# Attention of one graph with the other layers of its neighbours spread into its slots

## The chip, the cores and the metric

One Trainium2 chip; the program uses one of its cores. The metric is the device time of one execution in microseconds. Engines are named as in the profile: PE (TensorE; PEld its weight loads), DVE (VectorE), ACT (ScalarE), POOL (GpSimd), SP (SyncE, which here issues every DMA).

## What is computed

Sixteen graphs of N = 1024 nodes with D = 256 features go through two layers, each with a residual. `adj` holds 0 or 1 here (about 3% ones, and the diagonal), though the kernel also serves values up to 4.

```python
# layer 0: 8 heads of 32
h = maximum(layernorm(x), 0)
Q, K, V = h @ Wq.T + bq, h @ Wk.T + bk, h @ Wv.T + bv        # split into heads
A = softmax(where(adj == 0, -inf, Q @ K.T * HD**-0.5))       # per head, 1024 x 1024
x = x + concat(A @ V) @ Wo.T + bo
# layer 1: one "head", the score depends on the edge's kind
h = maximum(layernorm(x), 0)
e_k = leaky_relu((h * a_k) @ h.T, 0.2)                       # k = 0..3
s = where(adj == k + 1, e_k, ...), else -9e15
x = x + softmax(s) @ h
```

With ones only, `e_0` alone is needed. A flag per graph (is any entry above 1?) chooses at run time between that and a general path; on these inputs the general path is never taken.

## The kernel before

**Tiles.** A graph's attention is 64 tiles of 128 rows of scores by 1024 columns (8 heads x 8 row blocks; the order is four heads of a block, then the next block, and after 32 tiles the other four heads). Each tile is one *slot* of the loop in `layer0`: PE writes the scores into one of two PSUM tiles `ps` (`scores`, L837, two products over 96 rows: high and low parts of Q and K are stacked so that one product gives the split-precision sum); DVE adds the mask `bias` and takes the row minimum (`mask`, L510) into `sm`; ACT takes the exponential (L349); PE transposes the tile in eight pieces into `pT[0]` and `pT[1]` (L856); ACT copies the first half to `pt` (L359) and DVE the second (L525). `pt` has eight tiles (`SLOTS`). The attention values of a group of four tiles (64 weight loads and products, L873) are spread over four slots, a quarter behind the transposes of each (`values(t // HG - 1, t % HG)`). Scores run two slots ahead. Every 16 tiles (a quad) DVE forms row factors (L532, L535), PE transposes them (L884), ACT copies them (L365) and DVE scales the values into `ot` (L546).

**Order of a graph** (`graph`, L992 on PE, and the same on each engine, written out by hand): attention (`layer0`); transposes of the next graph's normalized `xf` (L778); `output` (L908, 32 products); the next graph's `front`: four products qk of twelve instructions (K and Q for heads 0 to 3, then for 4 to 7; L773), whose high parts ACT and low parts DVE write to a staging area in `pt` (L341, L469), and the value products; then `layer1`: h1 transposed (L778, L379, L592), and for each of eight tiles `edges` (12 products L773 of the row block scaled by a_0, whose parts L602, L387 and L611 make), DVE mask (L667) and leaky ReLU (L674), ACT exponential (L397), transposes (L963), copies (L403, L685), values with h1 (L975) and the result (L690, L693). `layer1` ends with the first two scores of the next graph.

**SP** issues in one queue: x1 and xf loads, the stacks (`stacks`, L220: 48 copies of staged parts into `ks` and `qs`), then adjacency halves (L208, 256 KB each, two buffers) for the next graph's masks beside layer 1, and the stores of the result.

**POOL** turns each adjacency half into `bias` with one pass (L290), adds the output bias to x1 (L308), and normalizes xf (`front_norm`, L297, L298, L302). **DVE** takes the maximum of every adjacency half (L483) for the flag. The next graph's statistics (L448) are taken on DVE in slots 22 to 30 of the attention.

## Time and profile before

| | |
|---|---|
| three runs, median (lowest to highest) | 3982.55 us (3978.19 to 3991.47) |
| profiled execution, span from first to last instruction (the page gives no other time of it) | 3976.3 us |
| mean granted TensorE clock | 0.967 |
| busy PE, DVE, ACT, POOL | 3669.7, 3128.6, 2267.1, 674.9 us |
| chain that ended last, by engine | PE 68%, SP queue 11%, issue 9%, DVE 7%, DMA 2%, ACT 1% |
| instructions | 94630 |

Busy time is the union of an engine's instructions. PE's is modelled at its ends, so a high share does not mean that PE works at its peak. "Issue" is time in which an engine waited for nothing that the profile shows. Of two consecutive instructions of one engine the second can start a little ahead of the end of the first, so what an instruction costs in a full queue is the distance of the two starts.

### The profile page before, as it was taken

The page shows a single profiled execution, that of the slowest core. Times are in us where ns is not written, and L with a number is a line of the kernel's source. Part 1 is how long each engine was busy: PE and PEld are TensorE (multiplying, and loading weights), DVE is VectorE, ACT ScalarE, POOL GpSimd, SP SyncE. Part 2 cuts the span into 40 slices and gives each one's busy share as a digit, 9 for nine tenths or more (in the row PEclk, how much of TensorE's full clock was granted, in tenths as well). Part 3 has the DMA queues.
Part 4 walks back from the last instruction along what each step waited for, and adds up shares of the span by engine and source line. Part 5 has one row for each costly group of instructions (what it writes and reads, how often), then busy time and mean ns, then how long its engine had stood idle before and what let it go on. Part 6 is the DMA issues. An engine that isn't in the chain of part 4 may idle for free.

```text
span 3976.3 us, 94630 instructions
## 1 busy us (share of the span) xinstructions
PE 3669.7 (92%) x34096; PEld 2908.9 (73%) x34096; DVE 3128.6 (79%) x5926; ACT 2267.1 (57%) x3940; POOL 674.9 (17%) x440
## 2 busy tenths in 40 slices
PE   6989989899998989989899898998989989899998
PEld 5777777777777767777777777776777767777776
DVE  6968778687886978869788696886968869688785
ACT  3837547275573845738456384663836638366482
POOL 1021030310303103031020301203012030120300
PEclk8999999999999999999999999999999999999999
DMA  5041220403204032040310503104031040311300
GB/s 151 2 105 36 60 82 2 117 25 70 71 2 118 23 76 66 2 131 10 81 61 4 137 2 83 59 15 126 2 89 53 21 121 2 95 47 31 99 2 12
DMA packets 129070, 227.67 MB, mean 57 GB/s; under 512 B 20672, under 2 KB 71104, under 8 KB 128448
## 3 DMA queue, kind: packets, MB, share of 16 engines
q1 hardware_dynamic: 128448, 219.50, 20.3%
q8 instruction: 376, 6.16, 0.7%
q14 instruction: 246, 2.02, 0.2%
HBM read 101.98 MB, written 16.78 MB: 30 GB/s over the span
## 4 chain that ended last, share of the span: by engine, by line
PE 68%; SPq 11%; issue 9%; DVE 7%; DMA 2%; ACT 1%; DVEq 0%; POOL 0%; POOLq 0%; ACTq 0%
PE pT L856 21%; PE ps L837 15%; PE pO L873 13%; SPq L220 11%; PE ps L773 8%; PE pO L975 7%; PE pT L908 2%; DMA adj_half<-in_adj_dram 2%; PE pT L963 2%; DVE pt L525 1%; DVE most L483 1%; DVE sm L667 1%; PE pO L884 1%; DVE sm L510 1%; DVE sm L674 1%
## 5 line engine op out<-in xcount | busy, mean ns | idle before, releaser
L349 ACT ACTIVATE sm<-sm,mn 128x1024 f32<-128x1024 f32 x1024 | 1179.5, 1152 | 454.8 <-DVE mn L510 452.5
L510 DVE CUSTOM_DVE_ANT_0 sm<-ps,bias 128x1024 f32<-128x1024 f32 x1024 | 1250.9, 1223 | 197.5 <-PE ps L837 178.0
L856 PE MATMUL pT<-ident,sm 128*128 128x128 f32 x8192 | 1098.6, 276 | 40.3 <-DVE pt L525 37.1
L856 PEld LDWEIGHTS pT<-ident,sm 128*128 128x128 f32 x8192 | 961.3, 142 | 218.5 <-DVE pt L525 52.8
L837 PE MATMUL ps<-ks,qs 96*128 96x512 f32 x2048 | 754.4, 451 | 4.6 <-issue 3.7
L525 DVE COPY pt<-pT 128x512 f32<-128x512 f32 x1024 | 702.4, 686 | 31.5 <-PE pT L856 30.8
L873 PE MATMUL pO<-pt,v 128*32 128x128 f32 x16384 | 649.7, 278 | 4.8 <-DVE pt L525 4.8
L359 ACT COPY pt<-pT 128x512 f32<-128x512 f32 x1024 | 583.2, 570 | 56.7 <-PE pT L856 56.4
L290 POOL TENSOR_SCALAR bias<-adj_half 128x512 bf16<-128x512 int32 x240 | 468.0, 1950 | 864.3 <-DMA adj_half<-in_adj_dram 855.7
L873 PEld LDWEIGHTS pO<-pt,v 128*32 128x32 f32 x16384 | 388.2, 109 | 170.1 <-issue 170.1
L975 PE MATMUL pO<-h,pt 128*128 128x256 f32 x2048 | 463.0, 379 | 0.0
L837 PEld LDWEIGHTS ps<-ks,qs 96*128 96x128 f32 x2048 | 312.6, 191 | 179.0 <-issue 168.9
L975 PEld LDWEIGHTS pO<-h,pt 128*128 128x128 f32 x2048 | 380.5, 190 | 47.5
L387 ACT ACTIVATE ah<-hs,nacol 128x128 fp32r<-128x128 f32 x256 | 87.0, 393 | 545.8 <-DVE hs L602 458.9
L773 PE MATMUL ps<-hh,ah 128*128 128x512 f32 x512 | 243.8, 476 | 161.1 <-DVE al L611 161.1
L773 PEld LDWEIGHTS ps<-hh,ah 128*128 128x128 f32 x512 | 111.7, 218 | 204.7 <-DVE al L611 181.6
L313 POOL TENSOR_TENSOR rstd<-vpe,mhalf 128x8 f32<-128x8 f32 x16 | 26.2, 1638 | 1294.3 <-DVE vpe L579 1294.3
L483 DVE TENSOR_REDUCE most<-adj_half 128x1 f32<-128x512 int32 x256 | 164.6, 678 | 95.0 <-DMA adj_half<-in_adj_dram 94.9
L773 PE MATMUL ps<-hl,ah 128*128 128x512 f32 x512 | 223.9, 437 | 0.0
L773 PE MATMUL ps<-hh,al 128*128 128x512 f32 x512 | 222.5, 435 | 0.0
L667 DVE CUSTOM_DVE_ANT_0 sm<-ps,bias 128x1024 f32<-128x1024 f32 x128 | 155.7, 1217 | 66.4 <-PE ps L773 66.4
L397 ACT ACTIVATE sm<-sm,mnl 128x1024 f32<-128x1024 f32 x128 | 147.1, 1149 | 91.3 <-DVE sm L674 91.3
(104 smaller groups left out, 3526.5 us busy)
## 6 DMA issues: line engine op xcount, KB each, us to landing
adj_half<-in_adj_dram SPq DMA_DIRECT2D x256, 256.0 KB, 2.8
ks<-pt SPq DMA_DIRECT2D x384, 128.0 KB, 2.4
qs<-pt SPq DMA_DIRECT2D x384, 128.0 KB, 2.4
xf<-in_x_dram SPq DMA_DIRECT2D x16, 1024.0 KB, 8.0
x<-in_x_dram SPq DMA_DIRECT2D x16, 1024.0 KB, 5.7
out_dram<-x SPq DMA_DIRECT2D x128, 128.0 KB, 2.9
x<-in_L_gnn_Wq_dram SPq DMA_DIRECT2D x1, 256.0 KB, 2.8
x<-in_L_gnn_Wk_dram SPq DMA_DIRECT2D x1, 256.0 KB, 3.1
```

The source lines that it names most:

```text
L220: sp.dma_start(dst[HD * row:HD * (row + 1), HG * (q // 2) + h, :].bitcast(F), stage[HD * h:HD * (h + 1), q, part, :].bitcast(F)).then_inc( ...
L290: nc.gpsimd.tensor_scalar(bias[:, t, c * HALF:(c + 1) * HALF], adj_half[:, c, :], 0.0, BIG, ALU.is_equal, ALU.mult).then_inc(mask_made, 1)
L349: nc.scalar.activation(sm[:, t % RING, :], sm[:, t % RING, :], ACT.Exp, scale=-1.0, bias=mn[:, t:t + 1], accum_out=den[:, t:t + 1]).then_i ...
L359: nc.scalar.copy(pt[:, t % SLOTS, 0:NT // 2, :], pT[0][:, :].rearrange("p (m n) -> p m n", n=P)).then_inc(pt_made[0], 1)
L483: nc.vector.tensor_reduce(most[:, i:i + 1], adj_half[:, i % 2, :], AX, ALU.max, apply_absolute_value=True).then_inc(adj_most, 1)
L510: nc.vector.tensor_tensor_reduce(out=sm[:, t % RING, :], in0=ps[t % 2][:, :], in1=bias[:, node, :], scale=1.0, scalar=3e38, op0=ALU.add, o ...
L525: nc.vector.tensor_copy(pt[:, t % SLOTS, NT // 2:, :], pT[1][:, :].rearrange("p (m n) -> p m n", n=P)).then_inc(pt_made[1], 1)
L773: last = nc.tensor.matmul(out, a, c, start=start and i == 0, stop=stop and i == len(terms) - 1)
L837: last = nc.tensor.matmul(ps[t % 2][:, c * HALF:(c + 1) * HALF], qs[:, head, node * P:(node + 1) * P], ks[:, head, c * HALF:(c + 1) * HALF ...
L856: last = nc.tensor.transpose(pT[c][:, j * P:(j + 1) * P], sm[:, t % RING, m * P:(m + 1) * P], ident[:, :])
L873: last = nc.tensor.matmul(pO[quad % 2][HD * h:HD * (h + 1), n], v[:, m, o:o + HD], pt[:, (HG * g + h) % SLOTS, m, :], start=(m == 0), stop ...
L975: last = nc.tensor.matmul(pO[t % 2][:, 0:D], pt[:, t, m, :], h1[:, m, :], start=(m == 0), stop=(m == NT - 1))
```

## The change

The kernel is reorganized so that a *stage* b is the attention of graph b, and all other work is cut into units that stand in its slots. On PE a slot is now: scores of tile s + 2; where it is due, a group's values (all 64 at once) and row transposes; the transposes of tile s; then the slot's unit, if it has one. Units share the two PSUM tiles `ps` with the scores in turn. For graph b itself: value products (slots 1, 2) and qk for heads 4 to 7 (4, 6). For the graph before, o = b - 1: output (3, 5), transposes of h1 (10, 11), and eight edge tiles (13, 17, ... 41), whose transposes follow three slots later ahead of the values of the group, and whose values stand in two halves ahead of the transposes of the two slots behind these. For the graph after: front transposes (53, 55) and qk for heads 0 to 3 (57, 58). DVE and ACT have the same slots; each engine's work on a unit stands behind its copy of the slot.

Buffers: `pt` has four tiles and one for layer 1 (before eight); h1 is `xf`; one PSUM tile `pA` holds the attention values, one, `pB`, row factors, layer 1 values and the flag; layer 1 has one `sm` slot and its own bias `gbias`. Adjacency is loaded twice per graph, for the masks and again for layer 1. The maximum on DVE is gone; POOL sums the excess over 1 instead. The sums L602 and the scalings L387, L611 per tile are replaced by one scaling of all of h per k. The relu of h1 is one ACT pass per block with the norm in it. Stacks are issued per head, for heads 4 to 7 of graph b behind slots 4 and 6, for heads 0 to 3 of the next behind slot 58.

```diff
-SLOTS = 8
+def background(earlier, later):
+    units = {1: ("value", 0), 2: ("value", 1), 4: ("qk", 2), 6: ("qk", 3)}
+    if earlier:
+        units.update({3: ("out", 0), 5: ("out", 1), 10: ("h", 0), 11: ("h", 1)})
+        units.update({13 + 4 * t: ("edge", t) for t in range(NT)})
+    if later:
+        units.update({53: ("front", 0), 55: ("front", 1), 57: ("qk", 0), 58: ("qk", 1)})
+    return units
...
-        pt = sb("pt", [P, SLOTS, NT, P], F)
+        pt = sb("pt", [P, HG + 1, NT, P], F)
...
# SP
+            def stack_heads(f, heads):
+                for h in heads:
+                    for q in range(2):
+                        dst = (ks, qs)[q]
+                        for row, part in enumerate(((0, 1, 0), (0, 0, 1))[q]):
+                            sp.dma_start(dst[HD * row:HD * (row + 1), h, :].bitcast(F),
+                                         parts[HD * h:HD * (h + 1), 2 * q + part, :].bitcast(F)
+                                         ).then_inc(stacked[h], 16)
+            def stage(b, later):
+                o, base = b - 1, 2 * NT * b
+                edge_adj(o, 0, base)
+                second_stack(b)
+                edge_adj(o, 1, base)
+                for t in range(NT - 3):
+                    edge_adj(o, t + 2, base)
+                    if t < NT - 4:
+                        store(o, t)
...
+                if later:
+                    mask_adj(b + 1, 3, base)
+                    sp.wait_ge(pv, NT * (o + 1))
+                    settle(sp)
+                    load_xf(b + 1, 0)
+                    load_xf(b + 1, 1)
+                store(o, 7)
...
+                load_x1(b)
+                if later:
+                    mask_adj(b + 1, 5, base)
+                    mask_adj(b + 1, 6, base)
+                    sp.wait_ge(s_mm, TILES * b + TILES // 2)
+                    settle(sp)
+                    first_stack(b + 1, (0, 1))
+                    mask_adj(b + 1, 7, base)
+                    stack_heads(b + 1, (2, 3))
# POOL
+            def masks(f, node, loaded):
+                for c in range(2):
+                    half = bias[:, node, c * HALF:(c + 1) * HALF]
...
+                        nc.gpsimd.tensor_scalar(half, adj_half[:, c, :], 1.0, 0.0, ALU.subtract,
+                                                ALU.max).then_inc(over_half, 1)
...
+                        nc.gpsimd.tensor_tensor(over[:, :], over[:, :], half, ALU.add).then_inc(over_sum, 1)
...
+                    nc.gpsimd.tensor_scalar(half, adj_half[:, c, :],
                                             0.0, BIG, ALU.is_equal, ALU.mult).then_inc(mask_made, 1)
+            def next_masks(f, node):
+                pool.wait_ge(masked, TILES * (f - 1) + TILES // 2 + HG * (node + 1))
...
+                masks(f, node, 2 * NT * (f - 1) + mask_load(node))
...
+                if later:
+                    next_masks(b + 1, 0)
+                    edge_bias(o, NT - 1, base + edge_load(NT - 1))
+                    for node in range(1, 5):
+                        next_masks(b + 1, node)
                     front_norm(b + 1)
+                    next_masks(b + 1, 5)
+                    residual(b)
+                    next_masks(b + 1, 6)
+                    next_masks(b + 1, 7)
# DVE, one slot
+                for s in range(TILES):
+                    if s + 2 < TILES:
+                        mask(b, s + 2, banks["score", s + 2], not earlier)
...
+                    if earlier and 16 <= s < 16 + 4 * NT and s % 4 == 0:
+                        edge_copy(o, (s - 16) // 4)
+                    if earlier and 19 <= s < 19 + 4 * (NT - 1) and s % 4 == 3:
+                        result(o, (s - 19) // 4)
...
+                    copy(b, s, not earlier)
+                    kind, n = units.get(s, ("", 0))
...
+                    if kind == "edge":
+                        edge_leaky(o, n)
+                    if s % 16 == 15:
+                        row_factors(b, s // 16, not earlier)
...
+                    if s and s % 16 == 0:
+                        norm(b, s // 16 - 1)
...
+                    if later and s in (48, 49):
+                        front_stats(b + 1, s - 48)
+                    if later and s == 49:
+                        front_aggregate(b + 1)
# PE, one slot
+                    if s + 2 < TILES or later:
+                        if s - 1 in units:
+                            pe.wait_ge(masked, TILES * b + s + 2)
+                        elif s - 2 in units:
+                            released(b, units[s - 2])
+                        else:
+                            pe.wait_ge(masked, TILES * b + s + 1)
...
+                    if earlier and 16 <= s < 16 + 4 * NT and s % 4 == 0:
+                        pe.wait_ge(pt_made[0], TILES * b + s)
+                        pe.wait_ge(pt_made[1], TILES * b + s)
+                        edge_transposes(o, (s - 16) // 4)
+                    if earlier and 18 <= s < 18 + 4 * (NT - 1) and s % 4 >= 2:
...
+                        edge_values(o, (s - 18) // 4, (s % 4 - 2,))
...
+                    if s and s % HG == 0:
+                        values(b, s // HG - 1, not earlier)
...
+                    transposes(b, s, not earlier)
+                    kind, n = units.get(s, ("", 0))
+                    if kind and s - 1 in units:
+                        released(b, units[s - 1])
+                    elif kind:
+                        pe.wait_ge(masked, TILES * b + s + 2)
+                    if kind == "value":
+                        value(b, n, banks["value", n])
...
# PE, the whole
+            stage(0, False, True)
             with pe.Fori(1, B - 1) as b:
-                graph(b, True)
+                stage(b, True, True)
+            stage(B - 1, True, False)
+            o = B - 1
...
+            edges(o, 0, 0, general)
+            for t in range(NT):
+                if t + 1 < NT:
...
+                    edges(o, t + 1, (t + 1) % 2, general)
...
+                edge_transposes(o, t)
+                edge_values(o, t, (0, 1))
```

`released` waits for the last reader of the unit's PSUM tile: for qk its low part on DVE, for h the low scaled part, for an edge tile its mask. `select`, the general path, is skipped by one branch per tile.

## Rows read from the trace of the kernel before

**Rows 1.** The page, part 1: busy time of each engine.

```profile
PE 3669.7 (92%) x34096; PEld 2908.9 (73%) x34096; DVE 3128.6 (79%) x5926; ACT 2267.1 (57%) x3940; POOL 674.9 (17%) x440
```

**Rows 2.** Windows: length, busy us of PE, PEld, DVE, ACT, POOL, clock, DMA share, GB/s.

```profile
0.00:62.00 62.00, 28.59 (x128) 24.28 (x128) 32.68 (x71) 9.58 (x10) 7.39 (x18) 0.81 0.55 157
1182.40:1428.10 245.70, 229.45 (x2130) 181.89 (x2130) 194.90 (x370) 141.54 (x246) 44.21 (x28) 0.97 0.21 58
1487.00:1494.00 7.00, 3.44 (x9) 2.73 (x10) 6.08 (x13) 2.30 (x5) 5.36 (x3) 0.52 0.27 83
3886.00:3976.30 90.30, 72.40 (x395) 60.92 (x384) 50.05 (x117) 23.60 (x45) 1.67 (x1) 0.91 0.04 14
```

**Rows 3.** Timeline of one attention slot and its neighbour. Columns: start us, us, engine.

```profile
1342.56 0.30 PEld L837 LDWEIGHTS ps<-ks,qs 96*128 96x128 f32 x2 [0.20 <-issue]
...
1342.91 1.02 PEld L856 LDWEIGHTS pT<-ident,sm 128*128 128x128 f32 x8
...
1343.52 1.23 DVE L510 CUSTOM_DVE_ANT_0 sm<-ps,bias 128x1024 f32<-128x1024 f32 x1
...
1344.10 0.38 PEld L873 LDWEIGHTS pO<-pt,v 128*32 128x32 f32 x16 [0.17 <-issue]
...
1344.67 0.69 DVE L525 COPY pt<-pT 128x512 f32<-128x512 f32 x1
1344.67 0.30 PEld L837 LDWEIGHTS ps<-ks,qs 96*128 96x128 f32 x2 [0.20 <-issue]
...
1344.79 1.15 ACT L349 ACTIVATE sm<-sm,mn 128x1024 f32<-128x1024 f32 x1 [0.36 <-DVE mn L510]
```

**Rows 4.** Timeline at the end of the same attention: last copy and value block.

```profile
1426.19 0.85 PEld L856 LDWEIGHTS pT<-ident,sm 128*128 128x128 f32 x8 [0.24 <-issue]
...
1427.32 0.69 DVE L525 COPY pt<-pT 128x512 f32<-128x512 f32 x1 [0.95 <-PE pT L856]
1427.93 0.24 DVE L532 RECIPROCAL rden<-den 128x16 f32<-128x16 f32 x1
1428.13 1.72 PEld L873 LDWEIGHTS pO<-pt,v 128*32 128x32 f32 x64 [0.54 <-issue]
...
1430.04 0.42 PEld L884 LDWEIGHTS pO<-ident,scratch 128*128 128x128 f32 x4 [0.20 <-issue]
```

**Rows 5.** Chain that ended last, one layer 1 step. Columns: start us, us.

```profile
1252.90 2.77 PE ps L773 x12
1255.68 0.87 PE pT L963 x8
1256.55 3.46 PE pO L975 x16
```

**Rows 6.** Groups of instructions by line, DVE and ACT, whole run.

```profile
L674 DVE SCALAR_TENSOR_TENSOR sm<-sm 128x1024 f32<-128x1024 f32 x128 | 156.0, 1219 | 0.0
...
L448 DVE BATCH_NORM_STATS2 st<-xf 128x6 f32<-128x256 f32 x128 | 52.9, 418 | 0.0
...
L379 ACT CAST hh<-ps 128x1024 fp32r<-128x1024 f32 x32 | 30.9, 1017 | 70.1 <-PE ps L778 70.1
```

**Rows 7.** Groups of instructions by line, POOL, whole run.

```profile
L290 POOL TENSOR_SCALAR bias<-adj_half 128x512 bf16<-128x512 int32 x240 | 468.0, 1950 | 864.3 <-DMA adj_half<-in_adj_dram 855.7
...
L302 POOL TENSOR_SCALAR xf<-xf,nmean,rstd 128x256 f32<-128x256 f32 x128 | 76.6, 611 | 3.5 <-POOL rstd L298 3.5
...
L308 POOL TENSOR_TENSOR x<-x,bob 128x2048 f32<-128x2048 f32 x16 | 73.2, 4574 | 209.6 <-DMA x<-in_x_dram 209.6
...
L298 POOL TENSOR_TENSOR rstd<-vpe,mhalf 128x8 f32<-128x8 f32 x16 | 26.7, 1666 | 0.0
```

**Rows 8.** Timeline of SP's queue: twelve stack copies, first to last issue.

```profile
1446.24 9.16 SPq L220 DMA_DIRECT2D ks<-pt  x12
```

**Rows 9.** The page, part 6: DMA issues, KB each, us to landing.

```profile
ks<-pt SPq DMA_DIRECT2D x384, 128.0 KB, 2.4
```

**Rows 10.** One line of the kernel: duration ns min/median/max.

```profile
L602 DVE TENSOR_TENSOR hs<-hh,hl x128: 410/419/832, 236.6 to 3950.1; 128x256 f32<-128x256 f32 x128
```

1451 lines of the change are left out of this document (771 added, 680 removed).

## The prediction

> **What bounds the kernel now.** The page's busy shares come first: PE is busy 92% of the span, DVE 79%, ACT 57%, POOL 17% [rows 1]. A busy share says little of where the time is lost, so I cut the run in windows. One graph takes 245.7 us; before the first graph's attention lie 62 us, after the last one's 90.3 us [rows 2]. The timeline of the attention shows a slot every 2.11 us, back to back on PE: scores .35, transposes 1.0 with a .17 gap behind them, a quarter of the values .38 and a .20 gap [rows 3]. So 64 slots are 135 us, bound by PE; DVE needs 1.75 of each slot (mask 1.15 from start to start, copy .60) [rows 3, 4], ACT about as much. The other 110 us of a graph are layer 1, whose steady step is 2.77 + .87 + 3.46 = 7.1 us on PE [rows 5], eight times 57 us, and output and front, 53 us in which PE has only some 31 us of work: four products of 2.77 (12 instructions of 512 columns, as the edges), 48 value instructions of half the width 5.7, 32 output instructions of .216 6.9 (3.46 for 16 of the same form), 32 transposes of .11 3.5, the row transposes 1.8, all from [rows 5] and the block in [rows 4]. The fourth window of [rows 2] shows what the waits there cost beside themselves: PE is busy 3.4 of 7 us and the granted clock is .52, the lower of the two levels (1.2 GHz). What the change can win is therefore at most the idle part of those 53 us.
>
> **The change, part by part.** The unit of account is one stage: 64 slots of attention with all units between. Constants, from start to start: S (scores) .35, T (transposes) 1.0, M (mask) 1.15, C (copy) .60; M can start .96 behind its S, the exponential 1.27 behind its M, C 1.13 behind its T [rows 3, 4].
>
> *Values in one lump.* pt shrinks from eight tiles to four and one for layer 1, and a group's 64 value instructions, before spread over four slots behind the transposes, now stand as one block ahead of the transposes of every fourth slot. On PE this is cheaper: 1.91 us as a block [rows 4] against four times .75. But the block needs all four copies, and the next copy needs the block. Four slots without a unit then are a ring: T to C 1.13, C .60, three times (M + C) 5.25, a hop of .2 (the block starts .81 behind the last copy's start), block 1.91, and .1 of waits: 9.2 us, where PE alone would need 4 x 1.35 + 1.91 = 7.3 and the kernel before takes 8.46. Cover is gone here: DVE has only one mask to do during the block.
>
> *Layer 1 in the slots.* A tile's step adds to four slots 2.77 of edges, 1.0 of transposes and 3.4 of values. PE sum: 4 x 1.35 + 1.91 + .17 + 2.77 + 1.0 + 3.4 = 14.6. Walking through the four slots, DVE (4 x 1.75, mask and leaky 2.4, copy and result 1.2 [rows 6]) is ready in time except for the last copy, on which the edge transposes wait .4. So 15.0 us, against 8.46 + 7.1 = 15.6 before. Eight times 15.0, two row transposes with their gaps 1.3, less .5 for the first tile: slots 13 to 44 take 121 us.
>
> *The other 32 slots.* I walked them in five stretches; each is the base of 9.2 per four slots or the PE sum, whichever is later, plus what is exposed.
> - Slots 45 to 52: base 18.4; the last tile's values 3.4; on DVE, which is the bound here, row factors .8, norm .6 (passes of the copy's size), eight statistics of .33 (.42 by their row [rows 6], overlapping by .09) 2.6, aggregates 1.0; the statistics stood at slots 22 to 30 before, in DVE's free .36 per slot. Sum 26.8.
> - Slots 53 to 58: base 13.8; two front transposes 2.0; two products qk 5.5; and a wait for POOL. POOL makes the next graph's masks with three passes per half where one was: two of 1.92 to 1.96 and a bf16 add of 512 columns that no row shows. The nearest rows bound it: 1.1 (a quarter of the 4.57 for 2048 columns) and 1.95 (the pass of the same size) [rows 7]; I take 1.2, as it is the same operation, and 5.2 per half with hops, 10.5 per node. Node 4 may start when slot 49's mask is done, 16.8 us into slot 45, ends at 27.4, and only then does front_norm follow (power 1.67 and small parts, 2.0, and four tiles of .61 [rows 7]): the front transposes of slot 53 can start at 31.9, PE is there at 27.9. Wait 4. Sum 25.3.
> - Slots 59 to 63 and slot 0: here SP is the bound. The stacks of the next heads are issued one after the other at .76 us (12 in 9.16 [rows 8]), 24 of them and two adjacency loads (1.2) behind the low parts of qk(1), the last lands 2.4 us later [rows 9]; the first needs 2.7 for the ACT and DVE passes on qk(1). 2.7 + 18.2 + 1.2 + 2.4 = 24.5. The jump back of the loop lies beside it.
> - Slots 1 to 6: PE sum 6 x 1.35 + 1.91 + values 5.7 + output 6.9 + qk 5.5 = 28.1, plus 2 of waits for the low parts (1.2, a pass of leaky's size [rows 6], behind ACT's 1.1) = 30.1.
> - Slots 7 to 12: base 13.8; both h units, each .9 on PE, two ACT passes of 1.02 [rows 6] and two DVE passes of 1.2, and each waited for before the next step: 11.2; the rest of qk(3) 1.2. Sum 26.2.
> Together 132.9. Walked slot by slot, some releases overlap with the base, 2.9 in all: 130.
>
> *What costs nothing.* Doubled adjacency loads (32 of 256 KB per stage): the DMA share is .21 [rows 2], and they go out between edges, 15 us apart. The vanished maxima, sums and scalings on DVE bring nothing either: DVE did them beside layer 1, where PE set the pace. Edge bias on POOL, 2 x 1.95, lies inside 15 us; if that cover went, the edge mask would be late. SP's second stack (24 issues, 18 us) ends just ahead of the scaled product in slot 10 that reuses its buffer.
>
> *Clock.* Waits of 4 us such as that of slot 53 stand in the trace ahead of stretches at 1.2 GHz; I add 1.7 for one such stretch. Nothing, and 5, are the ends.
>
> A stage: 121 + 130 + 1.7 = 252.7 us, where a graph takes 245.7. PE's own work falls to some 206 us (16 x 7.3, 57, 31), and it stands still for the other 47.
>
> *Ends.* Stage 0 has no layer 1; its masks are now POOL's alone, 10.5 us per node behind a slow SP queue, and it ends at 254 us (57 to the first slots instead of 62, masks of node 7 at 140, then 38 slots with the waits above). The last stage has no front: 22 less. The tail has one buffer for scores, values and copies in layer 1, so its step is T 1.0, copy .73, values 3.4, edges 2.77 = 7.9 for 7.1: 101 us instead of 90. Sum: 254 + 14 T + (T - 22) + 101 = 333 + 15 T = 4123 us with T = 252.7. The profiled execution has a span of 3976.3, the page gives no time around it, and the median of the runs is 6.3 us above it: **4130 us**, 3.7% slower.
>
> **Rivals.**
> 1. *PE stays the bound behind the block* (faster). If masks and copies keep up, for instance because PE's queue lets scores and transposes slip further ahead of DVE than I allow, four unit-free slots take 7.3 and not 9.2. Eight such groups: T = 252.7 - 15 = 237.5, total 3895 + 6 = 3900. It decides from T = 242.5 down, that is from 8.0 us per four slots. For it: the start-to-start times of M and C (1.75) fit into 2.11 with room; against it: DVE's ring is closed by the shrunken pt in the program itself, and at the end of each attention phase now, the block waits for the copy [rows 4]. Chance .20.
> 2. *The waits halve*: the transitions overlap better (units' low parts, POOL done earlier as its add is nearly free, stack DMAs earlier) and T lands at 242 to 243.5: no change, 3976 to 3988. Chance .05.
> 3. *POOL becomes the bound* (slower still). It works 44 us per graph now [rows 2] and would work some 135. TENSOR_TENSOR on DVE with both inputs in SBUF has a median of .419 but a longest of .832, [rows 10]: the two disturb each other already, rarely. If a half costs 7 in place of 5.2, the wait of slot 53 grows by 3.5, and the load ahead of the last stacks comes 6 later: T = 262, total 4270. Chance .13.
> The Trainium skill (SBUF, "Who interferes with whom") says that a DVE instruction with two SBUF inputs and a GpSimd instruction that reads SBUF exclude each other, the loser waiting for the whole instruction. By that rule each of the eight leaky passes could stand for a whole POOL pass and this rival would be the forecast. The trace bears it out only in part: the leaky pass of 1024 columns, two inputs in SBUF too, has a mean of 1219 ns over 128 [rows 6], beside POOL's mask passes of the same time.
> The forecast itself (ring of 9.2, T between 247 and 258, so 4045 to 4210) has .62.
> A further case, that the units do not run where the text puts them, I see no ground for: each engine's order is written out.
>
> **Numbers.** About .3%, 12 us, is what a measurement of this kernel can tell from no change. Faster .20, same .05, slower .75. The range takes the forecast's bounds, reaches down over half of rival 1 and rival 2, and up over most of rival 3: 3935 to 4240.
>
> **What would show it.** Right: in the new trace four unit-free slots (say 48 to 52 or 60 to 63) take over 9 us with V waiting on DVE's copy; four slots with an edge tile take near 15; PE waits for POOL's norm ahead of slot 53 and for stack DMAs at slots 63 and 0; value instructions stand in blocks of 64 in 1.9 us; PE's share falls under 88% in a longer span. Wrong: unit-free groups under 8 us; edge groups over 16 (then the layer 1 chain, not the transitions, is mis-sized); no wait at 53; a POOL busy share over 65%.

## The result and the profile after

The changed kernel takes 4325.2 us (median of 4 runs, 4319.3 to 4333.9) against 3987.0 for the kernel before on the same chip: 1.085 times as long, 95% interval 1.082 to 1.089. The forecast was 4130 us, range 3935 to 4240: the direction was right, the size 195 us short, and the result lies outside the range.

The page, part 1, of the changed kernel, to be held against [rows 1]:

```profile
span 4321.5 us, 94909 instructions
PE 3672.0 (85%) x34096; PEld 3013.0 (70%) x34096; DVE 2817.8 (65%) x4998; ACT 2245.5 (52%) x3812; POOL 2064.1 (48%) x1208
```

PE is busy for as long as before (3669.7), with the same number of instructions; DVE has 311 us less to do, POOL 1389 more. So PE stands for 343 of the 345 us more. The equal busy time hides two opposite things. By the trace's clock records PE was busy at 1.2 GHz, the lower of its two levels, for 28.6 us of a looped stage, and for 11.8 us of a graph before. An estimate from that, with matmuls that take twice as long at the lower level: at full clock PE would be busy for 213.5 us a stage where a graph took 222.9. The change did remove 9 us of work from the engine that bounds the kernel; the lower clock took 8 of them back (14.3 us for 5.9), and idle time grew by 18 (35.2 for 16.9).

I cut the run where DVE copies slot 0 of each stage (line L686). Stage 0 runs to 284.3, fourteen looped stages follow to 3967.2, 263.1 us each (of the kernel before, graph to graph: 245.7), and the last stage and the tail take 354.3. The windows of one looped stage, cut at the copies of slots 0, 6, 12, 16, 44, 48, 52, 58 and the next 0; the columns are those of [rows 2]:

```profile
1335.80:1367.00 31.20, 29.37 (x228) 24.83 (x226) 20.91 (x40) 12.41 (x21) 4.80 (x3) 1.00 0.25 59
1367.00:1391.20 24.20, 16.82 (x206) 13.69 (x206) 16.97 (x27) 18.36 (x31) 0.54 (x1) 0.93 0.36 89
1391.20:1409.10 17.90, 15.17 (x129) 12.21 (x128) 11.22 (x20) 9.03 (x17) 4.84 (x2) 0.81 0.10 32
1409.10:1517.70 108.60, 104.80 (x986) 87.89 (x985) 79.01 (x139) 60.84 (x107) 51.86 (x26) 1.00 0.15 49
1517.70:1530.30 12.60, 11.84 (x125) 9.71 (x124) 9.14 (x17) 7.35 (x14) 11.04 (x8) 1.00 0.44 132
1530.30:1545.00 14.70, 10.44 (x108) 7.92 (x106) 11.34 (x30) 6.90 (x13) 13.14 (x9) 0.77 0.42 131
1545.00:1570.10 25.10, 18.84 (x156) 15.29 (x155) 14.32 (x21) 13.20 (x22) 23.40 (x19) 0.86 0.10 32
1570.10:1598.80 28.70, 20.27 (x201) 15.63 (x200) 12.97 (x24) 11.94 (x20) 19.31 (x12) 0.82 0.58 140
```

Read the second and third column together. In slots 16 to 44, where layer 1 stands, PE is busy 104.8 of 108.6 us. PE stands 7.4 us in slots 6 to 12, 2.7 in 12 to 16, 4.3 in 48 to 52, 6.3 in 52 to 58 and 8.4 in the last row: most of its 35.4 idle us lie in the 32 slots without an edge tile. What PE waited for, over the whole run:

```profile
PE ps L966 <- DMA qs<-parts: 100.0, 39, 8.2
PE ps L921 <- POOL xf L402: 97.4, 16, 14.7
PE pT L978 <- DVE pt L686: 87.0, 52, 12.8
PE pT L978 <- ACT pt L486: 67.4, 32, 2.4
PE pT L1039 <- DVE pt L686: 54.1, 100, 0.9
PE pA L994 <- DVE pt L686: 51.4, 55, 1.1
```

Line, what was waited for, us in total, times, longest: scores wait for the stack copies, front transposes for POOL's norm (the longest, 14.7, is at the very first front; in the looped stages it is 5.3 on average), the transposes of a slot for the copies of the slot before. In the kernel before, the longest of these lists was PE waiting 161.1 us for the low part `al` in layer 1 (63 times); that is gone, and half a dozen new waits stand in its place.

The chain is broken off in this trace (it follows 2% of the span), so it is not used.

### The profile page after: what moved, and what is told of

The parts are those of the page before. It is cut to its first block and busy times, and to the rows that moved or that the text cites. A ratio compares the mean times of both kernels' runs of the same rounds, so it can differ in the third digit from the quotient of the medians.

```text
span 4321.5 us, 94909 instructions
## 1 busy us (share of the span) xinstructions
PE 3672.0 (85%) x34096; PEld 3013.0 (70%) x34096; DVE 2817.8 (65%) x4998; ACT 2245.5 (52%) x3812; POOL 2064.1 (48%) x1208
## 5 line engine op out<-in xcount | busy, mean ns | idle before, releaser
L676 DVE CUSTOM_DVE_ANT_0 sm<-ps,bias 128x1024 f32<-128x1024 f32 x1024 | 1246.7, 1217 | 119.5 <-PE ps L966 95.3
L978 PE MATMUL pT<-ident,sm 128*128 128x128 f32 x8192 | 1163.6, 285 | 161.3 <-DVE pt L686 87.0
L390 POOL TENSOR_SCALAR gbias<-adj_half 128x512 bf16<-128x512 int32 x256 | 590.0, 2305 | 1393.2 <-DVE mn L782 1310.5
L686 DVE COPY pt<-pT 128x512 f32<-128x512 f32 x1024 | 703.6, 687 | 543.8 <-PE pT L978 542.3
L994 PE MATMUL pA<-pt,v 128*32 128x128 f32 x16384 | 580.9, 301 | 58.9 <-DVE pt L686 51.4
L994 PEld LDWEIGHTS pA<-pt,v 128*32 128x32 f32 x16384 | 504.4, 122 | 151.2 <-issue 115.5
L364 POOL TENSOR_SCALAR bias<-adj_half 128x512 bf16<-128x512 int32 x240 | 466.1, 1942 | 257.2 <-DMA adj_half<-in_adj_dram 199.6
L371 POOL TENSOR_SCALAR bias<-adj_half 128x512 bf16<-128x512 int32 x256 | 497.4, 1943 | 49.4 <-POOL over L368 48.1
L1050 PE MATMUL pB<-xf,pt 128*128 128x256 f32 x2048 | 489.6, 384 | 6.7 <-ACT pt L517 4.2
L1050 PEld LDWEIGHTS pB<-xf,pt 128*128 128x128 f32 x2048 | 393.2, 192 | 72.9 <-ACT pt L517 6.3
L914 PE MATMUL ps<-hh,parts 128*128 128x512 f32 x1024 | 352.0, 405 | 5.4 <-DVE parts L659 5.2
L368 POOL TENSOR_TENSOR over<-over,bias 128x512 bf16<-128x512 bf16 x240 | 281.2, 1172 | 20.0
L914 PEld LDWEIGHTS ps<-hh,parts 128*128 128x128 f32 x1024 | 193.6, 189 | 50.4 <-issue 6.4
L1039 PE MATMUL pT<-ident,sm 128*128 128x128 f32 x1024 | 153.3, 298 | 73.4 <-DVE pt L686 54.1
```

Of the source, the lines that this page charges most:

```text
L364: nc.gpsimd.tensor_scalar(half, adj_half[:, c, :], 1.0, 0.0, ALU.subtract, ALU.max).then_inc(over_half, 1)
L371: nc.gpsimd.tensor_scalar(half, adj_half[:, c, :], 0.0, BIG, ALU.is_equal, ALU.mult).then_inc(mask_made, 1)
L390: nc.gpsimd.tensor_scalar(half, adj_half[:, c, :], 0.5, BIG, ALU.is_lt, ALU.mult).then_inc(adj_used[c], 1)
L676: nc.vector.tensor_tensor_reduce(out=sm[:, ring(t), :], in0=ps[i][:, :], in1=bias[:, node, :], scale=1.0, scalar=3e38, op0=ALU.add, op1=AL ...
L686: nc.vector.tensor_copy(pt[:, t % HG, NT // 2:, :], pT[1][:, :].rearrange("p (m n) -> p m n", n=P)).then_inc(pt_made[1], 1)
L914: last = nc.tensor.matmul(out, a, c, start=start and i == 0, stop=stop and i == len(terms) - 1)
```

## The experiments

Each run is given beside the kernel before, run on the same chip (3979.6 to 3990.6 us). The table has the medians; "stage" is the mean length of stages 1 to 14 in the profiled execution, and so are lengths of stretches of slots, where nothing else is said.

| run | us | ratio to before (95%) | stage 0 ends | stage |
|---|---|---|---|---|
| changed kernel | 4325.2 | 1.085 (1.082 to 1.089) | 284.3 | 263.1 |
| lump_four | 4233.5 | 1.064 (1.062 to 1.067) | | graph 261.1 |
| lump_eight | 4235.5 | 1.065 (1.062 to 1.067) | | graph 261.4 |
| no_excess | 4194.9 | 1.053 (1.051 to 1.056) | 250.8 | 256.6 |
| norm_first | 4267.2 | 1.072 (1.070 to 1.075) | 272.7 | 259.6 |
| early_front | 4239.7 | 1.063 (1.060 to 1.067) | 278.9 | 257.0 |
| fill_waits | 4347.2 | 1.088 (1.086 to 1.091) | 278.9 | 265.7 |
| fill_two (fill_waits again, one execution) | 4348.6 | | 284.2 | 264.8 |
| fill_three | 4312.2 | 1.081 (1.078 to 1.083) | 283.6 | 262.3 |
| act_order | 4309.4 | 1.080 (1.077 to 1.082) | 282.7 | 262.5 |
| split_block | 4337.4 | 1.087 (1.085 to 1.090) | 285.1 | 263.6 |
| quarters | 4420.9 | 1.109 (1.107 to 1.111) | 282.4 | 269.8 |
| early_act | 4235.5 | 1.061 (1.059 to 1.063) | 268.1 | 258.3 |
| early_quarters | 4297.7 | 1.077 (1.076 to 1.079) | 267.2 | 262.4 |
| stacks_ahead | 4362.0 | 1.094 (1.091 to 1.097) | 281.4 | 265.2 |
| tail_bias | 4319.1 | 1.083 (1.081 to 1.086) | 282.6 | 262.6 |
| tail_loads | 4297.3 | 1.078 (1.075 to 1.081) | 284.0 | 263.3 |
| best | 4217.2 | 1.058 (1.054 to 1.061) | 268.2 | 259.0 |

The looped stage is the same code in the changed kernel, tail_bias and tail_loads: 263.1, 262.6 and 263.3 us. It is the same code too in fill_waits and fill_two (265.7 and 264.8) and in early_front and best (257.0 and 259.0). So a stage that is 0.5 to 1 us shorter shows nothing by itself.

### The block of values alone, on the kernel before

```diff
-                    transposes(t)
-                    if t >= HG:
-                        values(t // HG - 1, t % HG)
+                    if t and t % HG == 0:
+                        for part in range(4):
+                            values(t // HG - 1, part)
+                    transposes(t)
```

lump_eight is this alone; lump_four also takes `pt[:, h]` and `pt[:, t % HG]` for the eight tiles, with the copies waiting for the group before.

> The kernel before, with one thing of the change alone: the values of a group of four slots stand as one block of 64 ahead of the transposes of the next group's first slot, and attention uses four pt tiles in place of eight, so that the first copy of a group waits for the block. Nothing else moves; layer 1 and the fronts stay where they were. My theory (the ring of copy, block, transposes, copy): four slots take 9.1 us in place of 8.46, so a graph takes 16 x 0.67 = 10.7 us more, 16 graphs 172 us: about 4159 us. Rival (the block is cheap on PE and hidden, the loss in the changed kernel comes from the units alone): 3990 us or less.

> As the run before it, but attention keeps its eight pt tiles: only the place of the value instructions is changed (one block ahead of the transposes of the next group's first slot). Theory A (the place in PE's order costs it: the block waits for the fourth copy and the next transposes stand behind the block): within 15 us of the run with four tiles, about 4150. Theory B, the one of my prediction's wording (the shrunken pt closes the ring): with eight tiles the copies run ahead and four slots go to 7.4 to 8.5 us, so 3720 to 4000.

Both take the same: 4233.5 and 4235.5 us, 254 and 256 above the 3979.6 of the kernel before. The copies on DVE in lump_four (timeline; start, us) show the ring; in the kernel before they stand 2.11 apart [rows 3]:

```profile
1219.92 0.69 DVE L525 COPY pt<-pT 128x512 f32<-128x512 f32 x1 [2.11 <-PE pT L856]
...
1221.67 0.69 DVE L525 COPY pt<-pT 128x512 f32<-128x512 f32 x1
1223.41 0.69 DVE L525 COPY pt<-pT 128x512 f32<-128x512 f32 x1
1225.15 0.69 DVE L525 COPY pt<-pT 128x512 f32<-128x512 f32 x1
1229.00 0.69 DVE L525 COPY pt<-pT 128x512 f32<-128x512 f32 x1 [1.14 <-PE pT L856]
```

Three times 1.74 and once 3.85: 9.08 us for four slots, as forecast (9.2). Two things follow. First, theory B, my own wording, falls: eight tiles bring nothing, since the next transposes stand behind the block in PE's queue anyway. It is the block's place that costs, not the shrunken `pt`. Second, the price is 16 us a graph (254 / 16) and not 10.7: the four-slot groups with row factors or a norm take 9.6 to 9.7, those with the statistics of the next front 10.0 to 10.8. Before, these DVE passes lay mostly in DVE's slack; in the ring most of each is added.

### Values in quarters again, in the changed kernel

```diff
-        pt = sb("pt", [P, HG + 1, NT, P], F)
+        pt = sb("pt", [P, 2 * HG + 1, NT, P], F)
-                    if s and s % HG == 0:
+                    if s and s % 16 == 0:
                         values(b, s // HG - 1, not earlier)
...
                     transposes(b, s, not earlier)
+                    if s % 16 >= HG:
+                        values(b, s // HG - 1, not earlier, (s % HG,))
```

The rest of the edit makes the room: qs and ks have six places for eight heads, so the scores of slots 32 to 63 are not those of the program, and on SP the stacks of heads 6 and 7 wait for those of 4 and 5.

> The changed kernel with the values back in quarters behind the transposes of four slots, in 12 of 16 groups (the group ahead of a row transpose keeps its block), and eight pt tiles for attention. The room comes from the stacked heads 4 to 7, which share two places in qs and ks: the scores of slots 32 to 63 are worked out from two heads in place of four, so their numbers are not the reference's; the same instructions run on the same shapes. Theory (the block of values costs every group that PE does not fill otherwise: 0.6 to 1.0 us in 8 of 16 groups of a stage, as the runs on the kernel before show, and stage 0): 16 x 6 = 95 less, about 4230 us; groups with an edge tile, which PE fills, stay at 15.4. Rival (in the stages with units, the units' own waits set the slots and the block is hidden): 4295 or more.

> The three exchanges and the values in quarters together (the scores of slots 32 to 63 from two heads in place of four, as said of the run with quarters alone). Theory (block and transitions are two separate costs, and add): 4212 - 95 = 4117 us, still 130 above the kernel before, because the groups with an edge tile are as long as before and the 32 other slots wait for the passes between units. Rival (without the block the waits between units fill, and the idea wins): under 3987 us.

The opposite came out: 4420.9 us, 96 slower than the changed kernel, and 4297.7 for the two together. By stretches of a stage, quarters wins where I looked for it only in part (slots 0 to 6: 30.0 for 31.3; 12 to 16: 16.9 for 17.5; 48 to 52: 12.9 for 14.8) and loses in the edge groups (slots 16 to 44: 115.4 for 108.7; 44 to 48: 14.6 for 12.6) and in slots 52 to 58 (26.8 for 25.4). Timeline of PE around the edge transposes (L1039) of the changed kernel:

```profile
1451.32 1.09 PE L1039 MATMUL pT<-ident,sm 128*128 128x128 f32 x8 [0.52 <-DVE pt L686]
1452.33 1.95 PE L994 MATMUL pA<-pt,v 128*32 128x128 f32 x64
1454.22 1.09 PE L978 MATMUL pT<-ident,sm 128*128 128x128 f32 x8
```

and of quarters (its edge transposes are L1046):

```profile
1445.73 1.09 PE L1046 MATMUL pT<-ident,sm 128*128 128x128 f32 x8 [0.52 <-DVE pt L689]
...
1447.65 1.06 PE L981 MATMUL pT<-ident,sm 128*128 128x128 f32 x8 [0.83 <-ACT pt L522]
1448.64 0.65 PE L999 MATMUL pA<-pt,v 128*32 128x128 f32 x16
```

In the changed kernel the block covers the copy of the edge transposes out of `pT`; without it PE stands 0.83 us. And a quarter costs .58 from start to start, four of them 2.3 where the block costs 1.89. The two together are 1.2 of the 1.6 us by which such a group is longer (17.0 for 15.4). So in groups that PE fills, the block is the better choice; the changed kernel's loss is not the block's loss.

### The block in two halves

```diff
                     transposes(b, s, not earlier)
+                    if s % HG == 0 and s % 16:
+                        values(b, s // HG - 1, not earlier, (0,))
```

The other half, whose tile part DVE writes, stays ahead of the transposes, and DVE's copy waits for that half alone.

> The changed kernel with the block of values in two halves in 12 of 16 groups: node blocks 4 to 7 ahead of the slot's transposes (DVE's copy waits for these alone), 0 to 3 behind them (ACT's copy waits for them). Theory (copy, block, transposes, copy is a chain with one length of PE behind each copy, and its place sets it): DVE's copy comes 0.9 earlier, the next slot 0.5, so 12 x 0.5 x 16 = 96 less, about 4230 us. Rival (ACT's copy then ends the wait at the same time): within 20 us of 4325.

No gain (4337.4, 12 more, and the intervals overlap). In an edge group DVE's copies stand 2.34, 5.04, 1.75 and 6.28 apart in the changed kernel, and 2.34, 3.73, 3.36 and 6.11 here: the copy behind the block comes 1.3 earlier, the next one later by more, 15.5 for 15.4 in all. The next transposes wait for ACT's copy too, and that one is released by the second half.

### POOL: its passes and their order

```diff
-                        nc.gpsimd.tensor_scalar(half, adj_half[:, c, :], 1.0, 0.0, ALU.subtract,
-                                                ALU.max).then_inc(over_half, 1)
...
-                        nc.gpsimd.tensor_tensor(over[:, :], over[:, :], half, ALU.add).then_inc(over_sum, 1)
+                        pool.sem_inc(over_sum, 1)
```

> The changed kernel without POOL's two extra passes per half (the sum of what the edge types exceed 1 by is left out but for the first half of each graph, so the flag is not really worked out). A node then costs POOL about 4.6 us in place of 11.35. If the wait for the front's norm is POOL's mask work, the wait of 5.2 at slot 53 goes in each stage, and stage 0, whose masks POOL paces, loses 25 to 30: 15 x 5.2 + 28 = 106 less, about 4220 us. Rival 1 (the stacks' DMAs hold the stage's end anyway and take the gain back): only stage 0 gains, 4295. Rival 2 (POOL's passes also slow DVE's everywhere): 4180 or less, with shorter DVE passes.

```diff
-                    for node in range(1, 5):
+                    for node in range(1, 4):
                         next_masks(b + 1, node)
                     front_norm(b + 1)
+                    next_masks(b + 1, 4)
```

The same exchange stands in stage 0.

> The changed kernel with one exchange in POOL's order: the front's norm stands ahead of node 4's masks, not behind them. Theory (POOL's order is what the front transposes wait for): the wait at slot 53 goes, node 4 to 7 have 10 us to spare until slot 14: 15 x 4.5 = 65 less, about 4260 us. Rival (the wait only moves to the stack DMAs at slots 63 and 0, or to late masks): less than 20 us of gain, 4305 or more.

no_excess takes 4194.9 us: 130 less, 33 of them in stage 0 and 6.5 in each looped stage, of which 6.4 in slots 52 to 58 (19.05 for 25.4). norm_first wins 58: slots 52 to 58 fall to 19.05 as well, but slots 58 to 64 rise from 28.0 to 31.3. The waits of PE for stack copies grow from 100 to 148 us, since by the program SP issues the stacks behind a mask load that waits for a node, which POOL now finishes later. The first step of the forecast's POOL term is thus shown, and the move of the wait too. DVE's passes are the same with POOL at 31% and at 48% (mask 1216 and 1217 ns), so rival 2 of that run falls. The groups of POOL in the changed kernel:

```profile
L390 POOL TENSOR_SCALAR gbias<-adj_half 128x512 bf16<-128x512 int32 x256 | 590.0, 2305 | 1393.2 <-DVE mn L782 1310.5 <-DMA adj_half<-in_adj_dram 64.2 <-POOL bias L371 9.5
L371 POOL TENSOR_SCALAR bias<-adj_half 128x512 bf16<-128x512 int32 x256 | 497.4, 1943 | 49.4 <-POOL over L368 48.1
L364 POOL TENSOR_SCALAR bias<-adj_half 128x512 bf16<-128x512 int32 x240 | 466.1, 1942 | 257.2 <-DMA adj_half<-in_adj_dram 199.6 <-POOL bias L371 50.7 <-DVE mn L676 6.8
L368 POOL TENSOR_TENSOR over<-over,bias 128x512 bf16<-128x512 bf16 x240 | 281.2, 1172 | 20.0
```

The bf16 add takes 1.17 us (taken: 1.2), a half 5.7 with its hops (5.2), a node 11.35 (10.5).

### The front earlier, ACT's order, the flag in stage 0

```diff
-        units.update({53: ("front", 0), 55: ("front", 1), 57: ("qk", 0), 58: ("qk", 1)})
+        units.update({51: ("front", 0), 53: ("front", 1), 54: ("qk", 0), 56: ("qk", 1)})
...
-                    mask_adj(b + 1, 6, base)
...
                     first_stack(b + 1, (0, 1))
+                    mask_adj(b + 1, 6, base)
+                    stack_heads(b + 1, (2, 3))
                     mask_adj(b + 1, 7, base)
-                    stack_heads(b + 1, (2, 3))
```

with POOL's order of norm_first.

> The changed kernel with the front a few slots earlier: POOL's norm ahead of node 4's masks, front transposes in slots 51 and 53, qk(0) in 54, qk(1) in 56 (for 53, 55, 57, 58), and on SP the stacks of heads 2 and 3 go out ahead of the last mask load. Theory (the end of a stage waits for POOL's norm and for the 24 stack issues, some 5 and 6 us a stage, and what they cost stands still for nothing else): both waits go, 15 x 11 = 165 less, about 4160 us. Rival (only the norm's wait can be won, what the stacks win is lost again in masks that come later or in the same passes of DVE): as the exchange on POOL alone, 4240 to 4267.

It wins 86 us, 28 more than norm_first alone, so the truth is nearer the rival. Slots 58 to 64 fall from 28.0 to 20.6, but 48 to 52 take 17.7 for 14.8 (the first front now meets the statistics on DVE), and a wait of up to 4.6 us ahead of the scores of head 2 is left, which the view puts down to the stack copies.

```diff
-                    if earlier and 14 <= s < 14 + 4 * NT and s % 4 == 2:
-                        edge_exp(o, (s - 14) // 4)
...
                     copy(b, s, not earlier)
+                    if earlier and 14 <= s < 14 + 4 * NT and s % 4 == 2:
+                        edge_exp(o, (s - 14) // 4)
```

> The changed kernel with one exchange on ACT: the exponential of an edge tile stands behind the copy of its slot, not ahead of it. Theory (on ACT, in order, the copy waits behind an exponential that waits for DVE's leaky pass, and the transposes of slots 15, 19, ... wait for the copy, up to 2.8 us): an edge group goes from 15.6 to 14.6 or less, 8 x 15 x 1 = 120 us less, 4205 us. Rival (PE is the bound of these groups, or DVE's chain is, and the edge transposes then wait for the later exponential): within 25 us of 4325.

The rival was right: 16 us less, of which 0.5 us a stage, no more than stages of the same code differ by. PE's waits for ACT's copy fall from 67.4 to 30.9 us, those for DVE's copy rise from 87.0 to 114.8, and an edge group still takes 15.4.

> The changed kernel with three exchanges together: the earlier front (4239.7 us alone), the edge exponential behind its slot's copy on ACT (16 us alone), and in stage 0 the reduction of the flag at slot 31 for 20, where DVE stood 13 us behind POOL's masks. If the three touch different waits: 4240 - 16 - 12 = 4212 us. Rival (they overlap, as they all shorten the same transitions, or POOL is late next): 4230 or more.

4235.5 us: stage 0 ends 10.8 earlier than in early_front (268.1 for 278.9), the rest gives nothing more. The waits overlap, as the rival had it.

### The clock

By the trace's clock records TensorE stood at 1.2 GHz, the lower level, for 642 us in the changed kernel and for 263 in the kernel before (35 us of a stage, 14 of a graph). Is that a cost, or only a sign that PE waits?

```diff
+            def filler(i, count):
+                for n in range(count):
+                    half = slice(n % 2 * HALF, (n % 2 + 1) * HALF)
+                    nc.tensor.matmul(ps[i][:, half], wvh[:, 0, 0:P], hh[:, n // 2 % 2, half], start=True, stop=True)
...
                     if kind == "front":
+                        if n == 0 and earlier:
+                            filler(banks["front", n], 12)
```

> The changed kernel with useless matmuls of 512 columns on PE inside four waits of each stage (12 ahead of the first front transposes, 4 and 12 ahead of the scores of the next graph's heads 1 and 2, 8 ahead of the first h transposes); their bank is overwritten by the real product behind them. They add 36 x 0.23 = 8.2 us of PE work to a stage, all of it where PE stood still. Theory (after such a wait the granted clock falls to 1.2 GHz for 3.4 to 6.8 us, 34 us of a stage, and the work there takes up to twice as long): the half-rate stretches fall under 20 us a stage and the time falls by 3 to 6 us a stage, 4235 to 4280 us. Rival 1 (the clock costs nothing, as other waits take up the slower passes): 4320 to 4330. Rival 2 (the filler is on the path): over 4340.

> A second look at the kernel with useless matmuls in four waits, for the spread of its own span: 4330 to 4365 us.

> The changed kernel with the useless matmuls only ahead of the front transposes and of the scores of the next graph's heads 1 and 2 (12, 4 and 12 of 512 columns), without those ahead of the h transposes, which cost 3 us a stage by themselves. Clock theory (half-rate stretches cost what the work in them lasts longer): the granted clock in slots 52 to 64 rises from 0.84 to 0.9, and the stage loses 1.5 to 3 us: 4285 to 4300. Rival, now mine (the waits behind absorb what the slower passes cost): 4320 to 4335, stage within 1 us of 262.9.

fill_waits was slower, 4347.2 us (fill_two, the same kernel once more, 4348.6): the eight fillers ahead of the h transposes lie on the path (slots 6 to 12 take 27.2 for 24.8). fill_three has no such place. Its time at 1.2 GHz falls by 140 us to 502, the work in those stretches could last up to 70 less, and the stage falls by 0.7 us, the whole by 13 (4312.2; by the ratios .5%, and the intervals overlap). tail_bias, whose stages have no filler, has 262.6 us a stage to fill_three's 262.3, so this is no clear gain. In fill_waits the last two rows of the stage read so:

```profile
1552.30:1578.00 25.70, 20.83 (x168) 16.62 (x167) 14.32 (x21) 13.22 (x22) 24.00 (x19) 0.93 0.10 31
1578.00:1606.70 28.70, 22.63 (x219) 17.95 (x218) 13.01 (x23) 11.77 (x20) 18.91 (x13) 0.88 0.58 140
```

The clock is .93 and .88 for .86 and .82, the length .6 more and the same. By this rival 1 of that run (the clock costs nothing) seems to hold. But the fillers are work too, 28 of .23 us or 6.4 us a stage, and they hide what the clock costs. In fill_three PE is busy 4.3 us longer in a stage and idle 5.0 us less: with the 2.3 us that the smaller time at 1.2 GHz gives back (an estimate, half of the 4.6 us less of busy time at that level), the fillers ate the gain.

What the lower clock costs can be read without fillers. The same four slots of fill_three, 12 to 16, in three of its stages (columns of [rows 2]):

```profile
3230.20:3245.50 15.30, 11.95 (x127) 9.63 (x127) 11.14 (x21) 8.82 (x16) 4.84 (x2) 1.00 0.11 37
2967.60:2984.50 16.90, 13.52 (x127) 10.89 (x126) 11.17 (x21) 8.84 (x16) 4.84 (x2) 0.90 0.11 33
2703.70:2721.60 17.90, 15.18 (x129) 12.17 (x128) 11.21 (x19) 8.97 (x17) 4.84 (x2) 0.81 0.10 32
```

With the same instructions and a clock of 1.00, .90 and .81 they last 15.3, 16.9 and 17.9 us, and PE is busy for 12.0, 13.5 and 15.2 of them: its own work lasts longer, so this is not only a longer wait. Over the 11 runs in which nothing of this stretch is changed, 154 stages, the two at full clock take 15.3 and 15.4 us, those at about .90 take 16.3 to 17.1 and those at about .81 take 17.6 to 18.0; the ranges do not meet. Slots 52 to 58 of early_front and best take 23.1 us at full clock and 24.5 to 24.7 at .93. The 64 instructions of a value block stand 1.68 us from first to last start at full clock and 3.2 at 1.2 GHz. So in these stretches the clock is a cost: rival 1 falls there, and the fillers alone could not tell. No run holds the clock at full level for the whole kernel, so the price of all 35 us stays an estimate.

### The end of a stage: DMA or the loop's jump

```diff
-                    mask_adj(b + 1, 5, base)
-                    mask_adj(b + 1, 6, base)
...
                     first_stack(b + 1, (0, 1))
+                    stack_heads(b + 1, (2, 3))
+                    mask_adj(b + 1, 5, base)
+                    mask_adj(b + 1, 6, base)
                     mask_adj(b + 1, 7, base)
-                    stack_heads(b + 1, (2, 3))
```

on top of early_front.

> The earlier front (4239.7 us), with all 24 stack issues ahead of the loads of masks 5 to 7 on SP. PE still stands 4.6 us ahead of the scores of head 2 at the stage's end there, put down to the stacks' DMA. Theory A (the DMA): the stacks land 3 to 9 us earlier, the wait goes, 15 x 4 = 60 less, about 4180 us. Theory B (the stage's end is the jump back of the loop, in which each engine stands some 3 to 5 us, and ACT's wait there has no releaser in the trace): the wait stays 4 us or more under another name, 4225 to 4250.

Theory B: slots 58 to 64 take 19.8 to 20.8 us, as in early_front (19.9 to 22.3). PE's timeline in the changed kernel, at the first scores behind the jump:

```profile
1591.93 1.22 PE L966 MATMUL ps<-ks,qs 96*128 96x512 f32 x2 [4.56 <-DMA qs<-parts]
```

and the same scores in stacks_ahead:

```profile
1597.16 0.91 PE L967 MATMUL ps<-ks,qs 96*128 96x512 f32 x2 [4.00 <-issue]
```

The copies for this head were all issued by 1592.42 there and land 2.4 us later, and PE still stands for 4.0, now for nothing that the trace names (48.8 us in 13 stages). Nothing else than the loop's jump back stands there in PE's program, and the traces hold two more signs of it. The loop runs 14 times and jumps back 13 times: the wait is there 13 times, and in the last pass slots 58 to 64 take 15.2 us where the other thirteen take 20.4 on average (early_front: 17.1 and 20.9). And in each of the 13 waits the DMA records have one transfer (of 23 in a stage) of 16 KB of instructions on queue q8, which starts 0.6 to 1.1 us behind PE's last instruction and ends 1.6 to 1.8 us ahead of its next one; from 1593 to 1598 us:

```profile
q8 instruction: 1, 0.02, 2.2%
```

In early_front the same transfer ends 1.6 to 1.8 us ahead of PE's next instruction, 13 times too, though the view names the stack copies there: so the wait is most likely the jump's there as well. In the changed kernel it ends 2.2 to 3.8 us ahead, and the copies that land later end the wait. No run takes the jump away, so this is strongly indicated and not isolated. The price of the order was seen too: 4362.0 us. With three mask loads, which wait for POOL's nodes, ahead of everything else on SP, the stacks of heads 4 to 7 are issued late, as the timeline of SP's queue in stacks_ahead shows:

```profile
1598.10 42.62 SPq L202 DMA_DIRECT2D adj_half<-in_adj_dram  x8
1641.02 7.50 SPq L226 DMA_DIRECT2D ks<-parts  x12
1648.79 8.19 SPq L226 DMA_DIRECT2D qs<-parts  x12
```

37 us into the stage for 22 in early_front, and the scaled h product of slot 10, which reuses their source, keeps ACT and then PE for up to 9 us (slots 6 to 12: 34.2 us for 25.5).

### The tail

```diff
-                    half = gbias[:, c * HALF:(c + 1) * HALF]
+                    half = (bias[:, t, :] if tail else gbias)[:, c * HALF:(c + 1) * HALF]
```

> The changed kernel, with the edge bias of the last graph's layer 1 (behind the last attention, the tail) written into the eight mask tiles, free by then, so that POOL does not wait for the mask pass of the tile before. The tail took 128 us in the changed kernel, 27 more than I forecast, with steps of 11 us for 7.9. Theory (load, POOL's two passes of 2 us or more, mask, leaky, exponential stand one behind the other in each step, since gbias is one buffer and has no attention beside it): steps fall to 8 to 8.5 us, 20 us less, about 4305. Rival (PE at its lower clock and ACT set the step): within 8 us of 4325.

4319.1 us, 6 less: the rival's number, but not its cause. POOL in tail_bias (two halves, start, us, idle before):

```profile
4245.06 3.92 POOL L392 TENSOR_SCALAR bias<-adj_half 128x512 bf16<-128x512 int32 x2 [7.16 <-DMA adj_half<-in_adj_dram]
4256.56 3.92 POOL L392 TENSOR_SCALAR bias<-adj_half 128x512 bf16<-128x512 int32 x2 [7.58 <-DMA adj_half<-in_adj_dram]
```

and SP's queue beside it:

```profile
4241.42 0.34 SPq L257 DMA_DIRECT2D out_dram<-x  x1
4241.95 0.82 SPq L202 DMA_DIRECT2D adj_half<-in_adj_dram  x2
```

The load waits in SP's queue behind the store of a result.

```diff
                 load_adj(B - 1, t, base + t)
-                if t:
-                    store(B - 1, t - 1)
-            store(B - 1, NT - 1)
+                if t >= 3:
+                    store(B - 1, t - 3)
+            for t in range(NT - 3, NT):
+                store(B - 1, t)
```

> The run with the tail's bias in the mask tiles, and on SP the stores of the tail's results three tiles behind the loads in place of one. In the run before, each load of the adjacency was issued 0.5 us behind a store that waits for the tile's result, and POOL stood 7 us a step for it. Theory (SP's in-order queue closes the tail's ring: result, store, load, POOL, mask, leaky, exponential): steps fall from 11.2 to 8 to 8.5 us, 7 steps, 20 us less than the run before: about 4299 us. Rival (load, leaky and exponential still set it, whatever SP does): 4312 or more.

4297.3 us. From the last copy of attention to the end it is 104.6 us now, 128.1 in the changed kernel; I had forecast 101.

> The changed kernel with what helped put together: front a few slots earlier and the stacks' order of the run early_front, the flag's reduction at slot 31 in stage 0, and the tail of tail_loads. Theory (stage 256.5, stage 0 some 208, tail 108): 4240 - 10 - 20 = 4210 us; still 220 above the kernel before, since 14 stages of 256.5 in place of 245.5 are 155 of it. Rival (the three give each other nothing back and the idea can be saved by order alone): under 4100.

4217.2 us: the best form of the change that still works out the flag, 108 less than the changed kernel and 233 more than the kernel before. (no_excess is lower, 4194.9, but leaves the flag's sum out; the two were not put together.) Its looped stages are the same code as early_front's, yet were longer (259.0 for 257.0): they had 33 us at 1.2 GHz for 27, and the execution profiled was the slowest of its four (4229.4 us), early_front's the fastest of its four (4232.6).

## Why the prediction was wrong

The sum stood at 4123 us for a span of 4321.5, 198.5 short: 30 in stage 0 (284.3 for 254), 145 in fourteen stages (263.1 for 252.7), 23 in the last stage and the tail (354.3 for 331.7). Most conditions of the forecast's own list held: blocks of 64 in 1.9 us (at full clock; 3.2 at the lower one), unit-free groups of 9.1 (they stand in stage 0 alone), edge groups of 15.3 to 15.7 (but the first one 17.5, over the 16 that the list calls wrong), a wait for POOL's norm at slot 53 and for the stacks at the end, PE under 88%.

**One step failed through the whole stage: the clock.** The prediction gave PE 206 us of own work in a stage and 47 in which it stands, and allowed 1.7 us for one stretch at 1.2 GHz. The trace has 35 us of a stage at that level, 28.6 of them with PE busy: by the estimate above 213.5 us of work at full clock, 14.3 for the lower level and 35.2 of standing. Where PE waits, the work behind stands at a lower clock (.81 in slots 12 to 16, .77 in 48 to 52, .86 and .82 in 52 to 64), and the constants of the sum all came from rows at a clock of 1.00. The other steps follow, point by point, from the stage at 1335.8 (in the mean over the stages slots 12 to 44 take 126.2 and 58 to 0 28.0):

- **Values in one lump**: 9.2 forecast, 9.13 measured (stage 0, slots 36 to 44). A quarter of the values was read as .75 us from [rows 3]; it is .58 from start to start, so the block saves PE 0.4 us a group and not 1.1. The reason given, the shrunken `pt`, was wrong: with eight tiles it is the same. The row factors, norms and statistics on DVE add to the ring; I had priced them in slots 45 to 52 only, and that stretch came out right (27.3 for 26.8).
- **Layer 1 in the slots**: PE sum 14.6 and a wait of .4 forecast; 14.88 and .52 measured, 15.40 in a plain group. With row transposes, and a first group of 17.9 in which the clock is .81, slots 12 to 44 take 126.6 for 121: **the first term mis-sized, 5.6 us a stage**. About 2.5 of them are the clock's: at full clock the same first group takes 15.3.
- **Slots 53 to 58**: 25.1 for 25.3. The wait for POOL was about 5 for 4, with a node of 11.35 for 10.5.
- **Slots 59 to 0**: 28.7 for 24.5, **the second, 4.2 us**. I counted 2.7 us from the copy of slot 58 to the first stack, and left out the product qk(1) that still stands in between on PE: 4.6 (copy at 1570.1, first issue at 1574.7); the 24 issues and the loads between took 20.8 for 19.4. "The jump back of the loop lies beside it" was true here, but it is the next bound, 4 us. The value blocks in this stretch took 3.0 and 3.6 us, at the lower clock.
- **Slots 1 to 12**: 55.3 for 56.3.
- **"Walked slot by slot, some releases overlap ..., 2.9 in all"**: this term had no row behind it, and nothing overlapped; **the third, 2.9 us**. Together 12.7, less .7 for the other stretches and the 1.7 of the clock, which is inside the measured rows: 10.3 of the 10.4.
- **Clock**: 1.7 allowed, 14.3 by the estimate, 8.4 more than in a graph before. It is no further item of the sum of 10.4: it lies inside the rows of the other points.
- **Stage 0**: POOL paces it, as said; **what failed is that I didn't ask which engine stands behind POOL there.** DVE takes the flag's reduction at slot 20, in its order, and stood 11.8 us for the sum over all nodes, with everything behind it:

```profile
134.21 0.69 DVE L686 COPY pt<-pT 128x512 f32<-128x512 f32 x1 [1.98 <-PE pT L978]
146.69 0.69 DVE L711 TENSOR_REDUCE most_all<-over 128x1 f32<-128x512 bf16 x1 [11.80 <-POOL over L368]
```

  and PE's wait for the norm at slot 53 was 8.3 us long there. Without POOL's excess stage 0 ends at 250.8.
- **Tail**: **a step of 7.9 forecast, 11 measured, the fourth term, 27 us.** I took PE's sum and the one-buffer chain of `ps` and `pT`; the ring that decided goes through SP (result, store, load, POOL's two passes, mask). "Edge bias on POOL lies inside 15 us; if that cover went, the edge mask would be late" named it, and in the tail the cover is gone. I did not use my own sentence there.

**The rivals.** Rival 1 (PE stays the bound behind the block, 3900) falls with the 9.1 us. Rival 2 (the waits halve) falls. Rival 3 had the right length of a stage (262) and the wrong mechanism: no POOL half took 7 us. Yet POOL's part is the largest single cost that a run took away: 130 us for the excess sum, which I had costed at the one wait of 4 and in stage 0's pace.

The Trainium skill (SBUF, "Who interferes with whom") has a two-input DVE pass and a GpSimd pass exclude each other. The trace agrees, and POOL is the loser: the leaky pass with two inputs in SBUF starts first and stays at 1218 ns, and 92 edge-bias passes that start beside it take 2.92 us where the 150 that do not overlap it take 1.92. The prediction looked at the leaky pass's time alone, which is the side that does not change. A pair of passes, the first beside the leaky pass:

```profile
1445.86 4.92 POOL L390 TENSOR_SCALAR gbias<-adj_half 128x512 bf16<-128x512 int32 x2 [10.41 <-DVE mn L782]
```

An edge group leaves POOL 15 us for it and it costs nothing in a stage: DVE's edge mask waits for POOL 7 times in the whole run (31.8 us), all of them in the tail.

**Why the idea does not pay.** Before, layer 1 had PE's whole time and attention had it nearly whole; only the 53 us of output and front had idle time, and in [rows 2] one graph leaves PE 16 us idle in all. That, and the 5.9 us that its lower clock costs by the estimate, was all there was to win. Spreading the units gave each its own wait for an ACT or DVE pass before the bank of `ps` came free, in slots whose scores and masks wait behind it. A stage leaves PE 35 us idle, and its clock stands at the lower level for 35 us where a graph had 14. Slots 12 to 44 take 126.6 where the same 32 slots and the eight steps of layer 1 took 124.5 before (32 x 2.11 and 57, the prediction's rows); the other 32 slots with output, front and h lose the remaining 15 of the 17.5 us by which a stage is longer than a graph was.
